# Moving the first pair of feed-forward products, three weight remainders and a table load ahead of the border between two parts of a decoder kernel

## What is computed

```python
def _qlinear(x, wq, scale):
    W = (wq.astype(jnp.float32) - ZERO_POINT) * scale[:, None]
    return jnp.einsum('bsd,hd->bsh', x, W)
gate = jax.nn.silu(_qlinear(x, wq_gate, s_gate))
up = _qlinear(x, wq_up, s_up)
return _qlinear(gate * up, wq_down, s_down)
```

## Time and profile before

| what | value |
|---|---|
| median of three runs | 1657.49 us (1656.73 to 1662.46) |
| the profiled execution's own time | 1660.14 us |
| its span, first to last instruction | 1658.4 us |
| mean granted TensorE clock | 0.992 of full speed |
| TensorE busy (matmul) | 1612.2 us, 97% |
| VectorE busy | 1161.4 us, 70% |
| ScalarE busy | 967.2 us, 58% |
| GpSimd busy | 548.9 us, 33% |
| border of the two parts | at about 1141 to 1142 us of the span |

### The profile page before, as it was taken

One profiled execution on the slowest core, in us unless ns is written; L12 is line 12 of the kernel. 1 busy time (PEld: TensorE's weight loads), 2 busy tenths in 40 slices (PEclk: granted clock), 3 DMA queues, 4 the chain that ended last, 5 costly groups with the idle time before them and its releaser, 6 DMA issues. The chain is left out here.

```text
span 1658.4 us, 42381 instructions
## 1 busy us (share of the span) xinstructions
PE 1612.2 (97%) x15332; PEld 1262.7 (76%) x15332; DVE 1161.4 (70%) x2087; ACT 967.2 (58%) x3876; POOL 548.9 (33%) x535
## 2 busy tenths in 40 slices
PE   6899999999999999999999999988999999999997
PEld 4677777777777777777777777766888888888885
DVE  7788888888888888888888888786644344444332
ACT  6477777777777776777777776774422222222221
POOL 4344443444444443444444444431011011011011
PEclk9899999999999999999999999998999999999999
DMA  6011111111110101111111111024221021120110
GB/s 218 29 32 32 37 30 55 30 30 37 47 38 30 37 30 55 30 30 37 43 42 30 37 30 40 17 72 149 93 77 50 27 76 33 43 76 25 51 51 26
DMA packets 55098, 81.00 MB, mean 49 GB/s; under 512 B 4880, under 2 KB 25488, under 8 KB 55056
## 3 DMA queue, kind: packets, MB, share of 16 engines
q1 hardware_dynamic: 55056, 80.43, 15.1%
HBM read 63.63 MB, written 16.78 MB: 48 GB/s over the span
## 5 line engine op out<-in xcount | busy, mean ns | idle before, releaser
L957 ACT ACTIVATE prob<-bank,nmax 128x128 f32<-128x128 f32 x1536 | 540.2, 406 | 146.3 <-DVE nmax L1209 142.5
L957 ACT ACTIVATION_READ_ACCUMULATOR prob<-bank,nmax 128x1 f32 x1536 | 377.1, 246 | 0.0
L1621 PE MATMUL fbank<-shared,piece_hi 128*128 128x512 f32 x1152 | 280.3, 394 | 0.0
L1209 DVE TENSOR_REDUCE nmax<-bank 128x4 f32<-128x512 f32 x376 | 233.5, 682 | 51.5 <-PE bank L537 42.7
L1621 PEld LDWEIGHTS fbank<-shared,piece_hi 128*128 128x128 f32 x1152 | 215.8, 187 | 53.2
L399 POOL TENSOR_TENSOR rope_buf<-rope_buf 128x512 f32<-128x512 f32 x128 | 165.7, 1304 | 128.1 <-DVE rope_buf L1162 128.0
L1773 DVE SCALAR_TENSOR_TENSOR h<-fbank,su_c,sil 128x512 f32<-128x512 f32 x88 | 65.9, 749 | 200.7 <-PE fbank L1621 197.2
L1707 ACT ACTIVATE sil<-fbank,sg_c 128x512 f32<-128x512 f32 x88 | 60.5, 688 | 175.4 <-PE fbank L1621 172.3
L1713 ACT ACTIVATE h_h<-h 128x512 fp32r<-128x512 f32 x88 | 55.6, 632 | 175.2 <-DVE h L1773 175.2
L449 POOL TENSOR_TENSOR cn_l<-cn,cn_h 128x512 fp32r<-128x512 f32 x64 | 82.8, 1294 | 204.0 <-DVE cn L1201 204.0
L513 PE MATMUL bank<-shared,z1T_h 128*128 128x512 f32 x520 | 141.4, 413 | 4.4 <-ACT shared L940 2.6
(11 more groups left out here) (181 smaller groups left out, 3167.8 us busy)
## 6 DMA issues: line engine op xcount, KB each, us to landing
xA<-in_x SPq DMA_DIRECT2D x32, 256.0 KB, 3.2
xB<-in_x SPq DMA_DIRECT2D x32, 256.0 KB, 3.1
x_scratch<-x SPq DMA_DIRECT2D x32, 256.0 KB, 2.0
shared_loaded<-x_scratch SPq DMA_DIRECT2D x8, 1024.0 KB, 7.7
xr<-x_scratch SPq DMA_DIRECT2D x8, 1024.0 KB, 5.6
out<-xr SPq DMA_DIRECT2D x8, 1024.0 KB, 4.3
cx<-in_ctx SPq DMA_DIRECT2D x32, 128.0 KB, 2.2
range_window<-in_wg SPq DMA_DIRECT2D x27, 112.0 KB, 2.0
```

Of the source, the lines that this page charges most:

```text
L957: last = nc.scalar.activation(prob[:, c, i, :], S[c][:, i * P:(i + 1) * P], ACT.Exp, bias=nmax[:, c, i:i + 1], accum_out=rs[:, h:h + 1])
L1209: nc.vector.tensor_reduce(out=nmax[:, c, :], in_=S[c][:, :].rearrange("p (g k) -> p g k", g=G), op=ALU.max, axis=AX, negate=True).then_inc ...
L1621: last = nc.tensor.matmul(dst[:, :], w[:, k, cols], z[:, k, :], start=(n == 0), stop=(n == len(passes) * KT - 1))
```

## The change

Four edits. (1) TensorE computes the first gate and up products (hidden tile 0) into banks 4 and 5 at the end of the attention part, behind project_o2(L); the second of them waits until VectorE has read bank 5 in add_cross(L). In the feed-forward part, in their place, stand two bare increments of the semaphores. With the flag at 1 the third pass is made there. (2) VectorE writes the low parts of the three weight pieces at the end of the attention part, behind add_cross(L). (3) ScalarE takes one silu of a constant column behind its last copy there, which puts the load of the activation's table ahead of the border. (4) The accumulator banks are allocated once for both parts, so that the products survive the border.

```diff
+        ffn["banks"] = [es.enter_context(nc.psum_tensor(f"bank{n}", [P, 512], fp32)) for n in range(8)]
...
                 ffn["some_low"] = pe.value_load(ffn["low_flag"][0:1, 0:1], min_val=0, max_val=1)
                 pe.wait_ge(x2_r, M + 1)
                 project_o2(L)
+                pe.wait_ge(f_zTh, KT)
+                pe.wait_ge(f_zTl, KT)
+                ffn_hidden(PA, 0)
+                pe.wait_ge(x2_r, L + 1)
+                ffn_hidden(PB, 1)
+
+            def ffn_hidden(dst, piece):
+
+                for n, z in enumerate((ffn["zT_h"], ffn["zT_l"])):
+                    for k in range(KT):
+                        nc.tensor.matmul(dst[:, :], ffn["hi"][piece][:, k, 0:P], z[:, k, :], start=(n == 0 and k == 0),
+                                         stop=(n == 1 and k == KT - 1))
...
                     nc.scalar.activation(ffn["zT_h"][:, k, :], FZ[k][:, :], ACT.Copy).then_inc(f_zTh, 1)
+                nc.scalar.activation(tables[:, 1:2], mhalf_c[:, 0:1], ACT.Silu)
...
-                    nc.vector.tensor_tensor(ffn["zT_l"][:, k, :], FZ[k][:, :], ffn["zT_h"][:, k, :], ALU.subtract)
+                    nc.vector.tensor_tensor(ffn["zT_l"][:, k, :], FZ[k][:, :], ffn["zT_h"][:, k, :], ALU.subtract).then_inc(f_zTl, 1)
                 add_cross(L)
+                for n in range(HEAD):
+                    nc.vector.scalar_tensor_tensor(out=ffn["lo"][n], in0=ffn["raw"][n], scalar=ZERO_POINT, in1=ffn["hi"][n],
+                                                   op0=ALU.subtract, op1=ALU.subtract)
...
+            def rest_of_hidden(dst, piece, done, low):
+
+                if not low:
+                    pe.sem_inc(done, 1)
+                    return
+                for k in range(KT):
+                    last = nc.tensor.matmul(dst[:, :], lo[piece][:, k, 0:P], zT_h[:, k, :], start=False, stop=(k == KT - 1),
+                                            skip_group_check=True)
+                last.then_inc(done, 1)
...
-                    hidden(GT[j % 2], "g", j, nb, low).then_inc(g_d, 1)
+                    if first and j == 0:
+                        rest_of_hidden(GT[0], 0, g_d, low)
+                    else:
+                        hidden(GT[j % 2], "g", j, nb, low).then_inc(g_d, 1)
...
-                    hidden(UP[j % 2], "u", j, nb, low).then_inc(u_d, 1)
+                    if first and j == 0:
+                        rest_of_hidden(UP[0], 1, u_d, low)
+                    else:
+                        hidden(UP[j % 2], "u", j, nb, low).then_inc(u_d, 1)
...
-            for n in range(HEAD):
-                nc.vector.scalar_tensor_tensor(out=lo[n], in0=ffn["raw"][n], scalar=ZERO_POINT, in1=hi[n],
-                                               op0=ALU.subtract, op1=ALU.subtract).then_inc(w_lo, 1)
+            dve.sem_inc(w_lo, HEAD)
             dve.wait_ge(cin, 48)
```

More of the change, by code:

```diff
@@ L209, in whole @@
             return LOADED[name][:, :, :]
-        bank = [es.enter_context(nc.psum_tensor(f"bank{n}", [P, 512], fp32)) for n in range(8)]
+        bank = ffn["banks"]
         S = bank[0:G]
@@ L263, in attention_phase @@
         rng_p, rng_row, rng_m, rng_flag = sem("range_partitions_ready"), sem("range_row_loaded"), sem("range_max_ready"), sem("low_flag_ready")
-        f_zT, f_zTh = sem("ffn_zT_done"), sem("ffn_zT_hi_ready")
+        f_zT, f_zTh, f_zTl = sem("ffn_zT_done"), sem("ffn_zT_hi_ready"), sem("ffn_zT_lo_ready")
         block = es.enter_context(nc.Block())
@@ L1526, in ffn_phase @@
         ve, r0, nt = sb("ve", [P, TPB]), sb("r0", [P, TPB]), sb("nt", [P, 4, TPB])
-        bank = [es.enter_context(nc.psum_tensor(f"fbank{n}", [P, 512], fp32)) for n in range(8)]
+        bank = ffn["banks"]
         DN = bank[0:TPB]
```

## The result

The changed kernel takes 1662.63 us, the median of 19 runs (1660.59 to 1667.86), against 1657.92 us for the kernel before (19 runs, 1654.93 to 1662.46). The ratio is 1.003 with a 95% interval of 1.0022 to 1.0038: slower by about 5 us (3.6 to 6.3). The profiled execution took 1661.55 us, its span is 1659.8 us and its mean granted clock 0.994. The span is only 1.4 us longer than that of before, although the medians differ by 4.7, because the attention part was 2.6 us shorter in this execution: the last residual sum (add_cross(L)) ends at 1138.55 us instead of 1141.11. That end lies anywhere from 1137.2 to 1142.3 us in the fourteen profiles of this study, the change or not.

A forecast was written before the change was run, and what follows sets the result against it. The prediction took TensorE to bound the feed-forward part, its first down product held by sd_b's landing. Border delay +3.49 and clock loss +1.3 made +4.8 us on the median 1657.49, so 1662.3 us, range 1657.0 to 1667.0.

The forecast's parts named there:

- First term: At the border: VectorE's moved low parts delay it, the loads behind it and the first down product; +3.49 us.
- The products: End of the attention part: the 16 moved matmuls by themselves delay the border 3.0 us or a little more.
- The table: ScalarE ahead of the border: the 1.28 us load is hidden there and was hidden before; the sum gets nothing.
- The first down product hangs on sd_b: Behind the border: silu waits for sd_b, landing in 5.19 us; the first down product then starts at 1154.60 us.
- Rival B: Silu ahead of the first down product: not held so tightly by sd_b, so faster, at best 1655.8 us; chance 0.07.
- Second term: TensorE at the first down product: after some 5.2 us of waiting its clock falls to half; +1.3 us.
- Rival A: TensorE ahead of the first down product: the clock holds, only the border's delay is left; +3.5 us, 1661.0; chance 0.22.
- Rival C: From the first down product on: a long fall of the clock, 5.1 us lost; +8.6 us, 1666.1; chance 0.11.

The follow-up runs named there:

- table alone: Only the early one-column silu on ScalarE, which loads the table ahead of the border, added to the kernel before; ratio 1.0007 (0.9998 to 1.0017).
- the split: sd_b on a semaphore of its own, so silu doesn't wait for it; against the kernel before, ratio 0.9992 in that kernel, 1.0012 in the changed one.
- products alone: The changed kernel without the moved low parts and the early table, so only 16 matmuls and common banks; ratio 1.0028 to the kernel before.
- Filling the wait: The changed kernel with 16 extra matmuls, their result overwritten, in TensorE's wait ahead of the first down product; ratio 1.0017 to the kernel before.
- sd_b last: sd_b on its own semaphore and issued behind the six weight pieces; against the kernel before, ratio 0.9992 in that kernel, 0.9999 in the changed one.

## Why the prediction was right

The forecast was +4.8 us and 1662.3 us; the runs gave +4.7 us by the medians and 1662.63 us. It named the mechanism, and the runs bear it out step by step: a later border, sd_b behind it, a longer wait, a fall of the clock. The sizes are less good than the sum. In the profile the first term is 1.1 us smaller than forecast and the second 0.3 us larger, 4.0 us together instead of 4.8; that the medians came within 0.4 us of the forecast is in part luck.

*First term, the border's delay: 3.49 us forecast, 2.4 us in the profile.* VectorE's low parts take 3.49 us and are last at the border, as predicted. They end 3.40 us behind the sum, as the first of them starts 0.09 us ahead of its end. But I took the 0.77 us from VectorE's end to the first issue as a fixed price of the border. In three kernels where VectorE or TensorE is clearly last it is 0.26 to 0.27 us. So before the change something else held the border 0.5 us longer than VectorE did, and the delay is 2.90 us. The store of x2 is what SyncE still does there: in the kernel before its issue ends at 1141.47 us, 0.41 us ahead of the first load. That it is the one was not tested. Of the rest 0.46 us are sd_b, which landed in 4.73 us instead of 5.19. I had thought of the x2 store as a cause, but with that store in its old place (table alone) it took 4.60, and in the changed kernel run again 5.10, with the store out of the way: the store doesn't decide it, and this load took from 4.4 to 5.2 us in the profiles where it is issued third.

*The products* would delay the border by 3.0 us, I said, and 2.39 us were measured with them alone; most of the gap between the two is again the 0.5 us. That VectorE and not TensorE sets the border is right, by 0.5 us.

*The table: nothing.* Right. The Trainium skill's larger price for a switch of tables ("ScalarE: Activation LUTs", What ACT_TABLE_LOAD costs) made no difference here, as all of it would lie beside the wait for sd_b; the row is 1.28 us for the load, and in the kernel before with the split, where nothing else holds silu, silu follows the load at once (1146.77 and 1146.78 us).

*The first down product hangs on sd_b.* Right, shown by the split: silu moved to the end of the table load in the kernel before, and to su_c's landing in the changed one. Rival B (faster) is out: sd_b took 4.73 us and not 2.0, and silu started 0.03 us behind it. Even with sd_b away the changed kernel is not faster, and what I had not seen is that the weight pieces stand right behind it as the next limit.

*Second term, TensorE's clock: 1.3 us forecast, 1.56 in the profile* (24 matmuls in 7.37 us instead of 5.81), 1.4 in the second profile of the kernel, 2.7 in the one with products alone. Filling the wait removed it. Rival A (the clock holds) is out for the profiles there are: it fell in all four with a wait of more than 4 us at this place or at the border, and in none of those with less. Rival C needed a fall of 9.6 us of dense work; the longest, with the products alone, was 6.8 us at half clock by its two-microsecond stretches, and not all of that was work. The Trainium skill ("TensorE: Matmul & The Clock Gate", HAM oscillation) tells of bursts of matmuls shorter than the DMA wait behind them, each next burst starting at half clock. The trace agrees: 3.91 us of matmuls, then 4.35 us of wait for what sd_b holds up, then the fall. The 2.96 us of the earlier trace rows, a wait for VectorE, were enough as well.

The sum of the profile is 2.4 + 1.6 = 4.0 us, a little below the 4.7 to 5.0 us of the runs. One profile catches one length of the fall, and the three with the moved products differ by 1.3 us. So the clock may make the difference, which is not shown. The prediction took 0.5% for the least difference that can be told from none; with 19 runs of each kernel the interval is 0.16% wide, and 0.3% stands clear of it.

## What to carry to other kernels

Work put ahead of a point where all engines meet is free only on the engine that is not last there, and it delays every load issued behind that point; ask first which load starts the next part, and load that earlier or wait for it later. Here the three weight low parts and sixteen matmuls cost nothing behind the border, beside the wait for sd_b, and moved the border by 2.4 to 2.9 us when put ahead of it. Taking one 256 KB load out of a shared wait and out of the way of the next loads brought the changed kernel back by 4 to 5 us. For the kernel before the same came out as 1.3 us, in an interval that still holds zero. And taking work out of a wait can cost on its own, if TensorE's clock falls in the longer wait.

## What was not expected

The two small scale vectors, kept in both parts and loaded early, came with a matmul spacing of 230 ns instead of 233 (3.68 and 3.73 us for 16), nearly all through the feed-forward part at a granted clock of 1.00. The profile has 6.0 us for it from the last residual sum to the end (509.5 instead of 515.5), of 8.6 us gained by the runs against the kernel before; some 1.3 of these belong to sd_b last, and the rest is open. The 32 matmuls of the first two tiles behind the border were not faster (7.52 us with and without). The sums over the whole run show which ones were, first with sd_b last, then with the small scales early as well (busy us, mean ns):

```profile
L1621 PE MATMUL fbank<-shared,piece_hi 128*128 128x512 f32 x1152 | 280.3, 394 | 0.0
L1621 PE MATMUL fbank<-shared 128*128 128x512 f32 x256 | 59.7, 390 | 1.7 <-PEq L142 1.7
```

```profile
L1625 PE MATMUL fbank<-shared,piece_hi 128*128 128x512 f32 x1152 | 276.4, 392 | 0.0
L1625 PE MATMUL fbank<-shared 128*128 128x512 f32 x256 | 59.7, 390 | 1.7 <-PEq L146 1.7
```

The hidden products whose weights are among the first three pieces, in the memory that both parts share, take the same time. Those whose weights lie in tiles of their own (piece_hi) take 3.9 us less. By the order of allocation in the kernel, these tiles are the ones that move in the feed-forward part, by the 88 bytes of the two vectors in each partition (2 x 11 x 4); the first three pieces stay, and so do the tiles that stood behind the vectors before. This fits the place of the tiles as the cause. But the attention part's weight tiles move too, and its matmuls on w_o_lo take 70.0 us instead of 70.1, so the place alone is not a rule. Whether it is the cause was not tested; a kernel that moves the tiles and loads nothing early would tell. Of the versions run, the kernel before with sd_b last and the small scales early is the fastest, 1648.59 us, 0.9948 (0.9934 to 0.9961) of the kernel before, and faster than both kernels of this study. The products ahead of the border add nothing to it.
